# Scaling the output and down weights by their gates on GpSimd instead of VectorE

## The reference

```python
h = _layernorm(x) * (1 + ca) + sa
x = x + ga * attn(h, ...)          # out = einsum('bth,oh->bto', rwkv, Wo) + bo
h = _layernorm(x) * (1 + cb) + sb
x = x + gb * ffn(h, ...)           # experts and shared: silu(h Wg) * (h Wu), times Wd
```

## Time and profile before

| | |
|---|---|
| median of three runs | 391.45 us (391.04 to 394.34) |
| profiled execution | 391.8 us, of which the span of its instructions is 390.0 us |
| busy in that span: TensorE matmul | 355.2 us (91%) |
| VectorE | 336.6 us (86%) |
| ScalarE | 286.7 us (74%) |
| GpSimd | 41.8 us (11%) |

### The profile page before, as it was taken

How to read it: one execution, slowest core, us unless ns; L and a number is a source line. 1 busy time by engine, 2 the same in 40 slices (tenths; PEclk the granted TensorE clock), 3 DMA queues, 4 the chain that set the end, 5 groups by cost and what they waited for, 6 DMA issues and landing times.

```text
span 390.0 us, 4478 instructions
## 1 busy us (share of the span) xinstructions
PE 355.2 (91%) x1461; PEld 254.6 (65%) x1461; DVE 336.6 (86%) x627; ACT 286.7 (74%) x446; POOL 41.8 (11%) x74
## 2 busy tenths in 40 slices
PE   3994592799999999999999999999999999989986
PEld 3942251468687758767766757776866767868765
DVE  5689999989999999999899999998999999851541
ACT  2579998878986899879885998699795987133210
POOL 3200006000400022002300040002300200010000
PEclk9879796699999999999999999999999999999999
DMA  8940020000003000102003000103010000100011
GB/s 274 257 146 3 0 68 26 0 2 1 0 2 108 0 1 2 54 2 72 22 2 109 0 2 0 54 3 94 0 50 6 0 1 2 54 0 2 0 54 55
DMA packets 16239, 14.87 MB, mean 38 GB/s; under 512 B 4766, under 2 KB 15192, under 8 KB 16216
## 3 DMA queue, kind: packets, MB, share of 16 engines
q1 hardware_dynamic: 16184, 14.58, 11.9%
q10 hardware_dynamic: 32, 0.01, 0.0%
HBM read 10.38 MB, written 4.21 MB: 37 GB/s over the span
## 4 chain that ended last, share of the span: by engine, by line
PE 47%; DVE 28%; ACT 12%; issue 7%; DMA 4%; POOL 1%; SPq 0%; DVEq 0%; ACTq 0%; POOLq 0%
PE mm L869 16%; PE yo L900 11%; PE mm L771 7%; PE yo L797 4%; DMA x_in<-in_L_attn_x_dram 3%; DVE state L1154 3%; DVE mixed L1136 3%; ACT arg L429 3%; DVE n_stats L1121 2%; PE tp L721 2%; ACT n_xn L364 2%; PE yo L909 2%; DVE act L1309 1%; DVE state L1173 1%; DVE state L1176 1%
## 5 line engine op out<-in xcount | busy, mean ns | idle before, releaser
L771 PE MATMUL mm<-mixed,WT 128*128 128x512 f32 x192 | 92.1, 624 | 5.7 <-DVE mixed L1136 5.7
L900 PE MATMUL yo<-WdG,act 128*128 128x256 f32 x320 | 70.8, 379 | 1.4 <-DVE act L1309 1.4
L771 PEld LDWEIGHTS mm<-mixed,WT 128*128 128x128 f32 x192 | 37.7, 202 | 45.6 <-issue 37.0
L900 PEld LDWEIGHTS yo<-WdG,act 128*128 128x128 f32 x320 | 60.2, 190 | 10.3 <-DVE act L1309 1.9
L869 PE MATMUL mm<-h_h,w_up_h 128*128 128x512 f32 x160 | 52.2, 407 | 0.0
L869 PE MATMUL mm<-h_h,w_up_l 128*128 128x512 f32 x160 | 50.4, 396 | 0.0
L869 PE MATMUL mm<-h_l,w_up_h 128*128 128x512 f32 x160 | 50.3, 395 | 0.0
L474 ACT ACTIVATE pool_g<-mm 128x512 f32<-128x512 f32 x40 | 23.6, 590 | 27.6 <-PE mm L869 27.5
L336 POOL TENSOR_TENSOR n_ve<-n_mv,small 128x4 f32<-128x4 f32 x16 | 5.3, 334 | 298.3 <-DVE n_mv L1125 298.3
L1136 DVE SCALAR_TENSOR_TENSOR mixed<-hT,cols,mixed 128x512 f32<-128x512 f32 x48 | 33.8, 746 | 1.3 <-ACT mixed L423 1.3
L869 PEld LDWEIGHTS mm<-h_l,w_up_h 128*128 128x128 f32 x160 | 30.0, 188 | 7.3
(11 more groups left out here) (160 smaller groups left out, 627.3 us busy)
## 6 DMA issues: line engine op xcount, KB each, us to landing
x_in<-in_L_attn_x_dram SPq DMA_DIRECT2D x8, 512.0 KB, 5.0
out_dram<-pool_x SPq DMA_DIRECT2D x5, 512.0 KB, 2.9
gate_rows<-gate_dram SPq DMA_DIRECT2D x4, 384.0 KB, 4.2
pool_x<-in_L_wmod_dram SPq DMA_DIRECT2D x2, 512.0 KB, 5.4
out_dram<-x_third SPq DMA_DIRECT2D x2, 512.0 KB, 3.2
pool_x<-in_L_wmod_dram SPq DMA_DIRECT2D x2, 256.0 KB, 4.4
pool_g<-in_L_ffn_Wg_dram SPq DMA_DIRECT2D x2, 256.0 KB, 4.9
pool_g<-in_L_ffn_Wu_dram SPq DMA_DIRECT2D x2, 256.0 KB, 4.0
```

Source lines behind the costliest of these rows:

```text
L771: last = nc.tensor.matmul(mm[PROJECT_BANK[j]][:, :], WT[:, w, kc, oc * P:(oc + 1) * P], mixed[:, w, kc, :], start=(kc == 0), stop=(kc == K ...
L900: last = nc.tensor.matmul(dst, act[:, e, t * P:(t + 1) * P], WdG[:, e, :], start=(e == 0), stop=(e == NB - 1))
```

## The change

The two functions move to GpSimd's stream. On VectorE only the bias step is left, under the name `bias_low`, with its waits on `rows_loaded` and `attn_mm`, at the places where `out_weight` stood; the four calls of `down_weight` (c0, c2, c4, c6) go without a replacement. On GpSimd the first pair runs behind `rstd` of norm 1 of c1; from then on `out_weight(c2, c4, c6)` runs behind the two `rstd` of n = 1, 3, 5, and `down_weight(c2, c4, c6)` behind those of n = 2, 4, 6. The list of SyncE is the same as before, and so are those of TensorE and ScalarE.

```diff
+            def out_weight(c):
+
+                b = c.batch
+                pool.wait_ge(rows_loaded, 16 * (b + 1))
+                wait(pool, attn_mm, KH * c.n)
+                if b == 0:
+                    pool.wait_ge(wo_done, 1)
+                nc.gpsimd.tensor_tensor(WoG[:, :, :], WT[:, O, :, :],
+                                        gate_rows[:, 0:1, :].to_broadcast([P, KH, H]), ALU.mult).then_inc(WoG_done, 1)
+
+            def down_weight(c):
+
+                b = c.batch
+                wait(pool, down_mm, KH * c.n)
+                if b == 0:
+                    pool.wait_ge(dn_in, 32)
+                nc.gpsimd.tensor_tensor(WdG[:, :, :], w_dn[:, :, :],
+                                        gate_rows[:, 1:2, :].to_broadcast([P, NB, H]), ALU.mult).then_inc(WdG_done, 1)
+
             rstd(norm1, chunk(0))
             rstd(norm1, chunk(1))
+            out_weight(chunk(0))
+            down_weight(chunk(0))
             for n in range(NC):
                 rstd(norm2, chunk(n))
                 if chunk(n + 2):
                     rstd(norm1, chunk(n + 2))
+                if n % 2 and chunk(n + 1):
+                    out_weight(chunk(n + 1))
+                elif n % 2 == 0 and n:
+                    down_weight(chunk(n))
...
-            def out_weight(c):
+            def bias_low(c):
...
-                if b == 0:
-                    ve.wait_ge(wo_done, 1)
-                nc.vector.tensor_tensor(WoG[:, :, :], WT[:, O, :, :],
-                                        gate_rows[:, 0:1, :].to_broadcast([P, KH, H]), ALU.mult).then_inc(WoG_done, 1)
                 ve.wait_ge(bias_high, b + 1)
...
-                nc.vector.tensor_tensor(WdG[:, :, :], w_dn[:, :, :],
-                                        gate_rows[:, 1:2, :].to_broadcast([P, NB, H]), ALU.mult).then_inc(WdG_done, 1)
...
-            down_weight(c0)
...
-            out_weight(c0)
+            bias_low(c0)
```

More of the change, by code:

```diff
@@ L1520, in _ @@
             divide(c2, 2)
-            out_weight(c2)
+            bias_low(c2)
             gate_up(c1, 0)
@@ L1539, in _ @@
                 prev, cur, nxt, after = (chunk(n + d) for d in (-1, 0, 1, 2))
-                down_weight(prev)
                 gate_up(prev, 3)
@@ L1561, in _ @@
                 divide(nxt, 2)
-                out_weight(nxt)
+                bias_low(nxt)
                 gate_up(cur, 0)
@@ L1579, in _ @@
             c4, c5, c6, c7 = (chunk(n) for n in (4, 5, 6, 7))
-            down_weight(c4)
             gate_up(c4, 3)
@@ L1601, in _ @@
             divide(c6, 2)
-            out_weight(c6)
+            bias_low(c6)
             gate_up(c5, 0)
@@ L1641, in _ @@
             residual1(c7, 0)
-            down_weight(c6)
             residual1(c7, 1)
```

## The result

The changed kernel takes 395.37 us in the median of 20 runs (393.38 to 397.69), the kernel before 391.83 us beside it (390.02 to 395.86). The ratio is 1.0084, with a 95% interval from 1.006 to 1.0108: slower by 0.8%, which is 3.3 us (the medians differ by 3.5). Each kernel's executions fall into a main group and a smaller one some 3 us above it (6 of the 20 of the kernel before took over 393 us), which is why these ranges are wide. The prediction said +0.6%. The profiled execution has a span of 392.5 us where the kernel before had 390.0 us; it took 394.3 us, 1.0 us less than the median of its kernel, while that of before stood at its median.

The account below looks back on a forecast made before the run. TensorE sets the pace from 75 to 350 us, VectorE's chain the startup. Terms 2.2 + 0.4 + 1.2 - 1.4 = +2.4 us against the 391.45 median give 393.9 us (+0.6%), range 387.3 to 398.5.

Parts of the forecast that it names:

- VectorE is held while GpSimd streams: Division of c0: VectorE's two-SBUF-input steps wait as long as GpSimd streams, losing 3.62 us; chance 0.45.
- The startup: Ahead of the full stretch: VectorE loses 3.62 us and gains 1.40, so +2.2 us, all on the chain.
- no hindrance: GpSimd does not hinder VectorE; 1.4 us at the start and 1.81 us of stalls gained: 388.2 us; chance 0.24.
- half speed: GpSimd and VectorE share the port where they meet, each slowed by half: about 391 us; chance 0.07.
- rival 3: VectorE keeps the port during two-input work and GpSimd starves; residual +2.0 us, less 1.8 later: 391.7 us; chance 0.07.
- The price of the products: On GpSimd, one pass over the data for each of two inputs: WoG 1.12 us, WdG 2.50 us.
- The clock: TensorE's half clock in startup idle time: a moved start can move the rise, allowed 1 us each way.
- WoG(c2), +0.4 us at 146.91: Behind `rstd` at 107 us, VectorE full: 1.12 us lost, 0.72 gained later; +0.4 us at the 146.91 us stall.
- WdG(c2, c4), +0.6 us each: About 157 and 242 us: VectorE loses 2.50 us, idle time and 1.17 us slack absorb part; TensorE stalls 0.6 each.
- The stalls that go, -1.4 us: Stalls at 200.69, 231.81 and 285.62 us vanish as VectorE regains WdG's 1.40 us and the x wait: -1.4 us.
- The bound behind the term: Behind 75 us, four TensorE waits over 0.4 us total 1.81, so VectorE relief gives back at most about 1.8 us.
- WdG(c6), 0: At 327 us, where VectorE waits for TensorE afterwards: the product costs 0.

Follow-up runs that it names:

- the spare products: Kernel before plus GpSimd products of the same sizes into spare buffers nobody reads, all real products left on VectorE: 401.24 us, ratio 1.0236.
- the copies: Kernel before plus eight spare one-input GpSimd copies of the same tiles, all products left on VectorE: 393.96 us, ratio 1.0043.

## Why the prediction was right

**VectorE is held while GpSimd streams.** Right: 3.53 us at the start against 3.62 in the sum. The startup was to be 2.2 us later; from the end of c0's sums to the statistics of norm 2 it is 2.07. (At the scan it is 2.01, so VectorE got 1.52 us back where 1.40 were counted.) The rivals of no hindrance and of half speed are refuted by the rows of 3.80 and 3.98 us and by the spare products. Starving GpSimd, rival 3, is wrong for the start, but between 159 and 163 us something like it happened.

**The price of the products.** Two passes was the right choice of the three. WoG was put at 1.12 us and takes 1.27 where nothing meets it; WdG was put at 2.50 and takes 2.92 to 3.17 us beside PSUM steps (the 3.17 with 0.3 us of waiting for VectorE's step under way). What it holds VectorE for is 2.57 and 2.76 us. The Trainium skill, "GPSIMD Engine Reference", section on elementwise side-by-side cycle accounting, led to an estimate of 2.81 us, which is nearer to the product's own rows and to the hold of 2.76 us than my 2.50; the hold of 2.57 us is nearer to 2.50.

**The clock.** It stood as an allowance of 1 us each way, not as a step. It is now 0.57 us in the profiled execution, and more where all of the projection runs at 1.2 GHz. This term was mis-sized, and it went for the slower side: the wait ahead of the projection grew from 1.81 to 4.54 us, and its matmuls from 3.62 to 5.08 us.

**WoG(c2), +0.4 us at 146.91.** The hold was there (1.01 us) and so were the 0.4 us, but not at that place: TensorE loses them bit by bit between 114 and 121 us, and the stall at 146.91 did not grow (0.42 us).

**WdG(c2, c4), +0.6 us each.** VectorE was held for 1.52 us rather than 2.50, because GpSimd streamed under the PSUM step and the idle time first; that idle time, 0.49 us, was not used up, as the sum had it, but is still there. TensorE lost 0.8 us each, so the slack behind was smaller than the sum's 1.17 us. The largest stall came at turn 2 (191.78 and 275.74 us, 0.48 and 0.47) and not at the spread of the routing weights.

**The stalls that go, -1.4 us.** That they go is right: 200.69, 231.81 and 285.62 are gone. The size is not: 1.7 and 1.1 us come back, 2.9 in all. The bound behind the term, that relief can give back at most 1.8 us, was wrong too: the kernel with WdG under PSUM steps gains 3.0 us between 163 and 332 us. The count of four waits over 0.4 us leaves out what is lost bit by bit, and one long wait inside the stretch, which stayed at 1.68 us in both kernels and so did no harm:

```profile
349.76 0.63 PE L721 MATMUL tp<-ident,n_xn 128*128 128x128 f32 x4 [1.68 <-DVE act L1309]
```

The loads of x come early, at 166.93 us and not at about 162, since WdG needs 7.16 us from its request.

**WdG(c6), 0.** Wrong: it costs TensorE 1.2 us, of which two small stalls show 0.47 and 0.36. It was not true that VectorE only waits there.

So behind turn 2 the sum had +0.2 us and the profile has +0.4. That they agree is luck: 1.5 us more came back than was counted, and WdG(c6) with 1.2 us and the other two WdG with 0.3 us more made up for it. It is luck too that the sum's +2.4 us is so near to the span's +2.5, for the latter has 0.53 us of head start in it. The total was 393.9 us against 395.37 measured; the kernel before took 391.83 us in the same runs, so of the 1.5 us of error 0.4 lie in the base, 0.6 in the clock, and the rest within what the runs can tell.

## What to carry to other kernels

Moving elementwise work with SBUF inputs from VectorE to GpSimd frees nothing while VectorE runs steps with two SBUF inputs: VectorE is held for as long as GpSimd streams, here 2.6 us for work that had cost it 1.4. Put such work under stretches in which VectorE reads PSUM or has one SBUF input, with a wait that starts it there, and check that VectorE's total busy time really falls (336.6 us before, 340.9 with the change, 332.0 with WdG under PSUM steps). In a trace the lost time hides inside the VectorE rows, so compare their durations with those of the same form elsewhere.

## What was unexpected

A request of GpSimd may be passed over at several ends of two-input steps: 7.16 us at 159.37 for a product that needs about 3, while at the scans (1.76 us) and between two division steps of the same form at 329.27 us it gets in at the first end. A one-input copy on GpSimd holds VectorE for little more than a third of what a product does (0.93 against 2.57 us for 1280 numbers). And in all four kernels that hold the division of c0 for 3.3 to 3.5 us TensorE did a part or all of the work behind it at 1.2 GHz (16 matmuls in 4.55 to 5.76 us in place of 3.62), so that the loss grows on an engine that had no part in it; where the hold was 1.0 us (the first WoG alone) or 1.2 us (the copies) they took 3.6 us.
